# First attention of a gated cross-attention block: a pair's output transposed and summed by one product

## The chip, the cores and the metric

The kernel runs on one core of a Trainium2 chip. Its time is that of one execution on the device, in microseconds. TensorE multiplies matrices, VectorE, ScalarE and GpSimd work on tiles of 128 partitions, and SyncE and GpSimd issue most DMAs.

## The reference

Four blocks follow each other on 4 x 512 tokens of 512 channels: a cross-attention with int8 fake-quantised projections (16 heads of 32 channels), a mixture of experts, a second cross-attention, and a quantised feed-forward net. Every block adds `tanh(gate)` times its output to `x`. The change is in the core of the first attention:

```python
q = q.reshape(B, N, H, Dh)        # N = M = 512 tokens, H = 16, Dh = 32
attn = jax.nn.softmax(jnp.einsum('bnhd,bmhd->bhnm', q, k) * scale, axis=-1)
o = jnp.einsum('bhnm,bmhd->bnhd', attn, v).reshape(B, N, C)
```

## The kernel before

`l0_projections` writes q and k to DRAM, each as a high part (fp32r) and the low rest, and v as both parts side by side. `l0_attention` then works in 16 groups (`NG`): a batch element and four heads (`HG0`) each. A group has `UN` = 16 steps, one for a head and a tile of 128 queries, so 256 steps in all; two heads are a *pair*, 8 steps, 32 pairs in all.

What a step does, by engine:

- TensorE: `scores` (one product of 128 x 512 over the stacked high and low parts), `transposes` of the (unnormalised) probabilities (four of 128 x 128, float32, by a product with the identity), `values` (two products of 512 columns, high and low part of the probabilities, accumulated in the bank `pO` over the 8 steps of a pair). The stationary operand `vT` of `values` holds 128 columns: for a pair's two heads the high and the low part of v, 32 columns each, the rest zeros.
- VectorE: `maxima` (the negated row maximum of the scores) and `low` (low part of the transposed probabilities).
- ScalarE: `exps` (exponential with the row sums) and `high` (the high part, from the bank).

At the end of a pair, ScalarE copies `pO` to `Os` (`o_copy`): 128 rows, which are 2 heads x 2 parts x 32 channels, by 512 queries. TensorE transposes it into the bank `pR` (`o_transposes`, line 910, four of 128 x 128). VectorE inverts the row sums (`reciprocal`, line 970) and adds the two parts with a reduction over `w` (line 972, in 128 x 512, out 128 x 256) into `osum`. GpSimd multiplies `osum` with the inverse row sums into `O` (`scale_pair`, line 827), and SyncE stores `O` once a group is done.

The order on each engine is written out by `pipeline(eng, N, 2 * UN, stages)`: in step s every stage (function, lag) handles item s - lag, in the order of the list, and a hardware loop runs over turns of 32 steps, that is 4 pairs. TensorE's list is `(transposes, 3), (scores, 0), (values, 9), (o_transposes, 10)`, ScalarE's `(high, 3), (exps, 1), (o_copy, 9)`, VectorE's `(low, 4), (maxima, 0), (sum_parts, 10)`. Engines are tied by semaphores (`flag`s): a value product at a pair's start waits until `pO` has been copied (`oT_done`), and at a group's start for V (`v_in`, `v_zeroed`) too; `scores` and `transposes` reuse three banks each (`SB`, `TB` = 3), and `reuse` gives the distance, which at the loop's wrap is two items, not three.

GpSimd's queue runs in order: for each group k it first scales the two pairs of group k - 1, then waits until the scores have reached group k (`s_done`), issues a DMA that writes zeros to `rows`, and in groups 1 to 6 also loads constants and expert weights of the next stage (`load_constants`, `load_weights`, lines 808 and 809) and splits them. SyncE loads the stacks of q and k for group n (`load_stacks`) once the scores of group n - 2 are done.

Of the kernel before, what the change touches and what calls it, by code (L numbers as in the profile page):

```python
# [11 lines left out]
ALU = mybir.AluOpType  # L12
ACT = mybir.ActivationFunctionType
AX = mybir.AxisListType.X
# [656 lines left out]
def l0_attention(nc, g, t, written, shared):  # L671
# [10 lines left out]
    with Mem(nc, "b") as m:  # L682
# [11 lines left out]
        osum = m.sb("o_sum", [P, 2, QT, 2, DH0])  # L694
# [6 lines left out]
        pR = m.ps("pR", [P, QT, P])  # L701
# [12 lines left out]
        oT_done, oTr_done, summed, o_done = m.flag("oT"), m.flag("oTr"), m.flag("summed", 2), m.flag("o_done", depth=4)  # L714
# [3 lines left out]
        zeroed, z_out, v_zeroed = m.sem("zeroed"), m.sem("z_out"), m.sem("v_zeroed")  # L718
# [68 lines left out]
        def pair_end(r):  # L787

            return r % (2 * QT) == 2 * QT - 1

        def pair_buffer(r):
            return r // (2 * QT) % 2

        @block.gpsimd
        def _(pool):
            for b in range(2):
                nc.gpsimd.memset(V[:, b, :, 1::3].bitcast(F32), 0.0).then_inc(v_zeroed, 1)
            nc.gpsimd.memset(Z[:], 0.0).then_inc(zeroed, 1)
# [22 lines left out]
            def scale_pair(np):  # L821

                gb, pair = np // PAIRS % 2, np % PAIRS
                pool.wait_ge(summed.sem, summed.done(np))
                if pair == 0:
                    pool.wait_ge(o_out[gb], 16 + np // (2 * PAIRS) * 16)
                nc.gpsimd.tensor_tensor(O[:, gb, :, 2 * pair * DH0:2 * (pair + 1) * DH0].rearrange("p k (h c) -> p k h c", h=2),
                                        osum[:, np % 2],
                                        rinv[:, np % 2].rearrange("p h k -> p k h").unsqueeze(3).to_broadcast([P, QT, 2, DH0]),
                                        ALU.mult).then_inc(o_done.sem, 1)  # L830

            for k in range(NG):
                for pair in range(PAIRS):
                    if k >= 1:
                        scale_pair((k - 1) * PAIRS + pair)
# [22 lines left out]
            for pair in range(PAIRS):  # L858
                scale_pair((NG - 1) * PAIRS + pair)
# [4 lines left out]
        def _(pe):  # L864
# [37 lines left out]
            def o_transposes(i, r):  # L902
                if not pair_end(r):
                    return
                np = i * 2 * PAIRS + r // (2 * QT)
                pe.wait_ge(oT_done.sem, oT_done.done(np))
                pe.wait_ge(summed.sem, summed.past(np, 1))
                m.wait_apart(pe)
                for k in range(QT):
                    last = nc.tensor.transpose(pR[:, k], Os[:, pair_buffer(r), bass.ts(k, P)],  # L910
                                               g["ident"][:])
                last.then_inc(oTr_done.sem, 1)
# [34 lines left out]
        def _(dve):  # L947
# [14 lines left out]
            def sum_parts(i, r):  # L962

                if not pair_end(r):
                    return
                np = i * 2 * PAIRS + r // (2 * QT)
                gb, h, q = place(r)
                head = gb * HG0 + h - 1
                dve.wait_ge(o_done.sem, o_done.free(np))
                nc.vector.reciprocal(rinv[:, pair_buffer(r)], rsum[:, head:head + 2]).then_inc(summed.sem, 1)  # L970
                dve.wait_ge(oTr_done.sem, oTr_done.done(np))
                nc.vector.tensor_reduce(osum[:, pair_buffer(r)], pR[:].rearrange("p k (h w c) -> p k h c w", h=2, w=2),
                                        axis=AX, op=ALU.add).then_inc(summed.sem, 1)

            pipeline(dve, N, 2 * UN, [(low, 4), (maxima, 0), (sum_parts, 10)])
# [2741 lines left out]
```

## Time and profile before

| | |
|---|---|
| time, median of 3 runs | 3120.47 us (3116.66 to 3122.2) |
| the profiled execution | 3125.14 us |
| its span, first to last instruction | 3123.4 us |
| mean granted TensorE clock | 0.973 |
| VectorE busy | 2315.6 us (74% of the span) |
| ScalarE busy | 2083.3 us (67%) |
| GpSimd busy | 1416.3 us (45%) |

The span is what the trace covers; the execution's own time is a little longer. In the rows below, PE is TensorE and PEld its weight loads, DVE VectorE, ACT ScalarE, POOL GpSimd, SP SyncE. Tiles of this stage begin with `b_`: `b_pR` is the bank of the transposed output, `b_oT` is `Os`, `b_o_sum` is `osum`. An engine's instructions may overlap at their ends, so a duration is longer than the distance between two starts.

### The profile page before, as it was taken

The page shows a single profiled execution, that of the slowest core. Times are in us where ns is not written, and L with a number is a line of the kernel's source. Part 1 is how long each engine was busy: PE and PEld are TensorE (multiplying, and loading weights), DVE is VectorE, ACT ScalarE, POOL GpSimd, SP SyncE. Part 2 cuts the span into 40 slices and gives each one's busy share as a digit, 9 for nine tenths or more (in the row PEclk, how much of TensorE's full clock was granted, in tenths as well). Part 3 has the DMA queues.
Part 4 walks back from the last instruction along what each step waited for, and adds up shares of the span by engine and source line. Part 5 has one row for each costly group of instructions (what it writes and reads, how often), then busy time and mean ns, then how long its engine had stood idle before and what let it go on. Part 6 is the DMA issues. An engine that isn't in the chain of part 4 may idle for free. (4 is left out here: it accounts for less than half of the span.)

```text
span 3123.4 us, 56345 instructions
## 1 busy us (share of the span) xinstructions
PE 2916.9 (93%) x15383; PEld 2376.0 (76%) x15414; DVE 2315.6 (74%) x4667; ACT 2083.3 (67%) x4262; POOL 1416.3 (45%) x1793
## 2 busy tenths in 40 slices
PE   6969997887999999899999899999999999899988
PEld 4657775776888877788888688888888888688755
DVE  5679998755777658767676289888998988734377
ACT  4469996422666546566666588888888888633366
POOL 3413101312001075367687377777777777442132
PEclk9989998998999999999999999999999999999999
DMA  6898663216888586545456532332322322195410
GB/s 196 271 216 197 163 171 102 78 56 234 289 258 282 170 285 208 156 143 171 142 169 186 162 96 73 99 94 76 99 91 79 99 90 80 49 322 183 163 40 34
DMA packets 401823, 474.32 MB, mean 152 GB/s; under 512 B 52276, under 2 KB 267220, under 8 KB 401652
## 3 DMA queue, kind: packets, MB, share of 16 engines
q1 hardware_dynamic: 388692, 419.72, 44.6%
q0 software_dynamic: 12960, 52.61, 5.0%
q8 instruction: 72, 1.18, 0.2%
q14 instruction: 99, 0.81, 0.1%
HBM read 304.30 MB, written 167.92 MB: 151 GB/s over the span
## 5 line engine op out<-in xcount | busy, mean ns | idle before, releaser
L2869 POOL TENSOR_SCALAR h_probs<-h_exp,h_rowsum_inv 128x512 f32<-128x512 f32 x512 | 359.0, 701 | 277.4 <-PE h_pT L2717 260.9
L2797 DVE TENSOR_REDUCE h_neg_max<-h_scores 128x1 f32<-128x512 f32 x512 | 349.3, 682 | 145.5 <-PE h_scores L2709 145.4
L2759 ACT ACTIVATE h_exp<-h_scores,h_neg_max 128x512 f32<-128x512 f32 x512 | 355.7, 695 | 110.6 <-DVE h_neg_max L2797 100.9
L2810 DVE TENSOR_TENSOR h_probsT_lo<-h_pT,h_probsT_hi 128x512 fp32r<-128x512 f32 x512 | 348.1, 680 | 0.0
L2717 PEld LDWEIGHTS h_pT<-ident,h_probs 128*128 128x128 f32 x2048 | 255.8, 141 | 71.5 <-POOL h_probs L2869 1.8
L2717 PE MATMUL h_pT<-ident,h_probs 128*128 128x128 f32 x2048 | 307.3, 272 | 0.9 <-POOL h_probs L2869 0.8
L2768 ACT CAST h_probsT_hi<-h_pT 128x512 fp32r<-128x512 f32 x512 | 301.1, 588 | 0.9 <-PE h_pT L2717 0.9
L2985 PE MATMUL k_acc<-k_w_hi,k_cat 128*128 128x512 f32 x512 | 200.9, 392 | 12.3 <-POOL k_w_lo L3066 11.4
L2732 PE MATMUL h_pO<-h_probsT_hi,n_lo 128*128 128x512 f32 x512 | 203.3, 397 | 0.0
L2986 PE MATMUL k_acc<-k_w_lo,k_cat 128*128 128x512 f32 x512 | 200.4, 391 | 0.0
L925 ACT ACTIVATE b_probs<-b_scores,b_neg_max 128x512 f32<-128x512 f32 x256 | 184.2, 719 | 14.6 <-DVE b_neg_max L952 14.6
L952 DVE TENSOR_REDUCE b_neg_max<-b_scores 128x1 f32<-128x512 f32 x256 | 173.6, 679 | 20.4 <-PE b_scores L874 20.4
L2971 ACT CAST k_cat<-k_cat 128x512 fp32r<-128x512 bf16 x128 | 79.2, 621 | 161.5 <-PE k_acc L2986 143.3
L2554 DVE TENSOR_TENSOR g_normed<-g_pQ,g_rstd 128x512 f32<-128x512 f32 x160 | 110.2, 689 | 96.1 <-PE g_pT L2458 89.6
L934 ACT CAST b_probsT_hi<-b_pT 128x512 fp32r<-128x512 f32 x256 | 156.1, 610 | 29.4 <-PE b_pT L882 29.4
L959 DVE TENSOR_TENSOR b_probsT_lo<-b_pT,b_probsT_hi 128x512 fp32r<-128x512 f32 x256 | 173.5, 678 | 0.0
L2588 POOL TENSOR_TENSOR g_rstd<-g_var_eps,neg_half 128x4 f32<-128x4 f32 x160 | 166.3, 1039 | 13.5 <-POOL g_var_eps L2586 0.2
L2856 POOL TENSOR_TENSOR n_lo<-n_raw,n_hi_second 128x512 fp32r<-128x512 f32 x128 | 165.5, 1293 | 0.0
L882 PE MATMUL b_pT<-ident,b_probs 128*128 128x128 f32 x1024 | 156.1, 275 | 3.7 <-DVE b_probsT_lo L959 2.4
L2856 POOL TENSOR_TENSOR n_lo<-n_raw,n_hi_first 128x512 fp32r<-128x512 f32 x120 | 155.3, 1294 | 0.0
L882 PEld LDWEIGHTS b_pT<-ident,b_probs 128*128 128x128 f32 x1024 | 125.8, 142 | 38.8 <-issue 8.5
L2494 ACT ACTIVATE g_squares<-g_pQ 128x512 f32<-128x512 f32 x160 | 95.4, 597 | 83.8 <-PE g_pQ L2448 77.5
(460 smaller groups left out, 9051.3 us busy)
## 6 DMA issues: line engine op xcount, KB each, us to landing
e_w_raw<-in_w SPq DMA_DIRECT2D x24, 1792.0 KB, 8.1
lnT<-g_out SPq DMA_DIRECT2D x160, 256.0 KB, 2.3
n_raw<-lnT SPq DMA_DIRECT2D x64, 512.0 KB, 5.1
e_w_raw<-in_w SPq DMA_DIRECT2D x24, 896.0 KB, 9.9
n_raw<-lnT SPq DMA_DIRECT2D x64, 256.0 KB, 5.3
n_raw<-v SPq DMA_DIRECT2D x64, 256.0 KB, 5.6
cat<-h_cat SPq DMA_DIRECT2D x128, 128.0 KB, 1.8
k_cat<-cat SPq DMA_DIRECT2D x128, 128.0 KB, 4.4
```

Source lines behind the costliest of these rows:

```text
L882: last = nc.tensor.transpose(pT[r % TB][:, k], Pr[:, r % 4, bass.ts(k, P)], g["ident"][:])
L925: nc.scalar.activation(Pr[:, r % 4], pS[r % SB][:], ACT.Exp, bias=nmax[:, r % 4:r % 4 + 1], accum_out=rsum[:, gb * HG0 + h, q:q + 1]).then ...
L2717: last = nc.tensor.transpose(pT[r % 4][:, k], Pn[:, r % 4, bass.ts(k, P)], g["ident"][:])
L2732: nc.tensor.matmul(pO[h][:], vl, PTh[:, br * HPG + h, k], start=False, stop=(k == QT - 1)).then_inc(o_mm.sem, 1)
L2759: nc.scalar.activation(Pr[:, r % 4], pS[r % 2][:], ACT.Exp, bias=nmax[:, r % 4:r % 4 + 1], accum_out=rsum[:, r % 4:r % 4 + 1]).then_inc(ex ...
L2768: nc.scalar.copy(PTh[:, br * HPG + h, :, bass.ts(q, P)], pT[r % 4][:]).then_inc(hi_done.sem, 1)
L2797: v.tensor_reduce(nmax[:, r % 4:r % 4 + 1], pS[r % 2][:], axis=AX, op=ALU.max, negate=True).then_inc(nmax_done.sem, 1)
L2810: v.tensor_tensor(PTl[:, br * HPG + h, :, bass.ts(q, P)], pT[r % 4][:], PTh[:, br * HPG + h, :, bass.ts(q, P)], ALU.subtract).then_inc(lo_ ...
L2856: nc.gpsimd.tensor_tensor(Lo[:, gb, slot], Raw[:, gb, slot], Hi[gb][:, slot], ALU.subtract).then_inc(op_lo.sem, 1)
L2869: nc.gpsimd.tensor_scalar(Pn[:, r % 4], Pr[:, r % 4], rinv[:, r % 4:r % 4 + 1], 1.0, ALU.mult, ALU.mult).then_inc(norm_done.sem, 1)
L2985: nc.tensor.matmul(bank[:], lhsT, Wh[:, k], start=(k == 0), stop=False)
L2986: ins = nc.tensor.matmul(bank[:], lhsT, Wl[:, k], start=False, stop=(k == CK - 1))
```

## The change

The bank `pR` becomes half as wide, `[P, QT, 2, DH0]`. In place of four transposes TensorE makes four products (`nc.tensor.matmul`) of the same stationary operand with `fold`, a 128 x 64 float32 matrix: two identities of 32 for each head, one above the other, so that the product transposes and adds the two parts. `fold` is made once by GpSimd (a memset and two `affine_select`). `osum` and the reduction go. VectorE's `invert` computes the reciprocal at lag 8, and its new `scale_pair` at lag 10 multiplies `pR` with it straight into `O`. GpSimd no longer scales; the rest of its queue is as before. TensorE's wait before the products is now for the scaling of the pair before, and once for `fold`.

```diff
--- before.py
+++ after.py
@@ -691,14 +691,14 @@
         PTh = m.sb("probsT_hi", [P, HG0, QT, S], F32R)
         PTl = m.sb("probsT_lo", [P, HG0, QT, S], F32R)
         Os = m.sb("oT", [P, 2, S])
-        osum = m.sb("o_sum", [P, 2, QT, 2, DH0])
+        fold = m.sb("fold", [P, 2, DH0])
         nmax = m.sb("neg_max", [P, 4])
         rsum = m.sb("rowsum", [P, 2 * HG0, QT])
         rinv = m.sb("rowsum_inv", [P, 2, 2, QT])
         pS = [m.ps(f"scores{j}", [P, S]) for j in range(SB)]
         pT = [m.ps(f"pT{j}", [P, QT, P]) for j in range(TB)]
         pO = m.ps("pO", [P, S])
-        pR = m.ps("pR", [P, QT, P])
+        pR = m.ps("pR", [P, QT, 2, DH0])
 
         qk_in = [m.sem("qk_in0"), m.sem("qk_in1")]
         qk_first = m.sem("qk_first")
@@ -711,11 +711,11 @@
         s_done, nmax_done, tr_done = m.flag("scores"), m.flag("nmax"), m.flag("tr", depth=4)
         exp_done, hi_done, lo_done, o_mm = m.flag("exp", depth=6), m.flag("hi"), m.flag("lo", depth=6), m.flag("o_mm", depth=16)
 
-        oT_done, oTr_done, summed, o_done = m.flag("oT"), m.flag("oTr"), m.flag("summed", 2), m.flag("o_done", depth=4)
+        oT_done, oTr_done, inverted, o_done = m.flag("oT"), m.flag("oTr"), m.flag("inverted"), m.flag("o_done", depth=4)
         QK_LOADS = 8
         ZR = ROWS // NG
         Z = m.sb("zero", [P, ZR * D // P])
-        zeroed, z_out, v_zeroed = m.sem("zeroed"), m.sem("z_out"), m.sem("v_zeroed")
+        zeroed, z_out, v_zeroed, folds = m.sem("zeroed"), m.sem("z_out"), m.sem("v_zeroed"), m.sem("folds")
         block = m.block()
 
         def where(i, r):
@@ -795,6 +795,11 @@
         def _(pool):
             for b in range(2):
                 nc.gpsimd.memset(V[:, b, :, 1::3].bitcast(F32), 0.0).then_inc(v_zeroed, 1)
+            nc.gpsimd.memset(fold[:], 0.0).then_inc(folds, 1)
+            for part in range(2):
+                pool.wait_ge(folds, part + 1)
+                nc.gpsimd.affine_select(out=fold[:], in_=fold[:], compare_op=ALU.not_equal, fill=1.0, base=-part * DH0,
+                                        pattern=[[-2 * DH0, 2], [-1, DH0]], channel_multiplier=1).then_inc(folds, 1)
             nc.gpsimd.memset(Z[:], 0.0).then_inc(zeroed, 1)
             pool.wait_ge(zeroed, 1)
             rows = t["rows"].rearrange("n d -> (n d)")
@@ -818,21 +823,7 @@
                 pool.wait_ge(c_hi, k + 1)
                 nc.gpsimd.tensor_tensor(shared.c_low[:, k], Cr[:, k % 2], shared.c_high[:, k], ALU.subtract).then_inc(shared.c_lo, 1)
 
-            def scale_pair(np):
-
-                gb, pair = np // PAIRS % 2, np % PAIRS
-                pool.wait_ge(summed.sem, summed.done(np))
-                if pair == 0:
-                    pool.wait_ge(o_out[gb], 16 + np // (2 * PAIRS) * 16)
-                nc.gpsimd.tensor_tensor(O[:, gb, :, 2 * pair * DH0:2 * (pair + 1) * DH0].rearrange("p k (h c) -> p k h c", h=2),
-                                        osum[:, np % 2],
-                                        rinv[:, np % 2].rearrange("p h k -> p k h").unsqueeze(3).to_broadcast([P, QT, 2, DH0]),
-                                        ALU.mult).then_inc(o_done.sem, 1)
-
             for k in range(NG):
-                for pair in range(PAIRS):
-                    if k >= 1:
-                        scale_pair((k - 1) * PAIRS + pair)
                 pool.wait_ge(s_done.sem, s_done.depth + max(k * UN, UN // 2))
                 pool.dma_start(rows[k * ZR * D:(k + 1) * ZR * D].rearrange("(p a) -> p a", p=P), Z[:]).then_inc(z_out, 16)
                 if k == 1:
@@ -855,8 +846,6 @@
                                             ALU.mult, ALU.mult).then_inc(folded, 1)
                     nc.gpsimd.tensor_scalar(shared.bp[:], shared.bp[:], g["tanh_gates"][:, 0:1], 1.0,
                                             ALU.mult, ALU.mult).then_inc(folded, 1)
-            for pair in range(PAIRS):
-                scale_pair((NG - 1) * PAIRS + pair)
             pool.wait_ge(folded, 2)
             pool.wait_ge(z_out, 16 * NG)
 
@@ -904,11 +893,12 @@
                     return
                 np = i * 2 * PAIRS + r // (2 * QT)
                 pe.wait_ge(oT_done.sem, oT_done.done(np))
-                pe.wait_ge(summed.sem, summed.past(np, 1))
+                pe.wait_ge(o_done.sem, o_done.past(np, 1))
+                pe.wait_ge(folds, 3)
                 m.wait_apart(pe)
                 for k in range(QT):
-                    last = nc.tensor.transpose(pR[:, k], Os[:, pair_buffer(r), bass.ts(k, P)],
-                                               g["ident"][:])
+                    last = nc.tensor.matmul(pR[:, k].rearrange("p h c -> p (h c)"), Os[:, pair_buffer(r), bass.ts(k, P)],
+                                            fold[:].rearrange("p h c -> p (h c)"), start=True, stop=True)
                 last.then_inc(oTr_done.sem, 1)
 
             pipeline(pe, N, 2 * UN, [(transposes, 3), (scores, 0), (values, 9), (o_transposes, 10)])
@@ -959,7 +949,7 @@
                 nc.vector.tensor_tensor(PTl[:, h, :, bass.ts(q, P)], pT[r % TB][:],
                                         PTh[:, h, :, bass.ts(q, P)], ALU.subtract).then_inc(lo_done.sem, 1)
 
-            def sum_parts(i, r):
+            def invert(i, r):
 
                 if not pair_end(r):
                     return
@@ -967,12 +957,23 @@
                 gb, h, q = place(r)
                 head = gb * HG0 + h - 1
                 dve.wait_ge(o_done.sem, o_done.free(np))
-                nc.vector.reciprocal(rinv[:, pair_buffer(r)], rsum[:, head:head + 2]).then_inc(summed.sem, 1)
+                nc.vector.reciprocal(rinv[:, pair_buffer(r)], rsum[:, head:head + 2]).then_inc(inverted.sem, 1)
+
+            def scale_pair(i, r):
+
+                if not pair_end(r):
+                    return
+                np = i * 2 * PAIRS + r // (2 * QT)
+                gb, h, q = place(r)
+                dve.wait_ge(inverted.sem, inverted.done(np))
                 dve.wait_ge(oTr_done.sem, oTr_done.done(np))
-                nc.vector.tensor_reduce(osum[:, pair_buffer(r)], pR[:].rearrange("p k (h w c) -> p k h c w", h=2, w=2),
-                                        axis=AX, op=ALU.add).then_inc(summed.sem, 1)
-
-            pipeline(dve, N, 2 * UN, [(low, 4), (maxima, 0), (sum_parts, 10)])
+                if h == 1:
+                    dve.wait_ge(o_out[gb], 16 + i * 16)
+                nc.vector.tensor_tensor(O[:, gb, :, (h - 1) * DH0:(h + 1) * DH0].rearrange("p k (h c) -> p k h c", h=2), pR[:],
+                                        rinv[:, pair_buffer(r)].rearrange("p h k -> p k h").unsqueeze(3).to_broadcast([P, QT, 2, DH0]),
+                                        ALU.mult).then_inc(o_done.sem, 1)
+
+            pipeline(dve, N, 2 * UN, [(low, 4), (maxima, 0), (invert, 8), (scale_pair, 10)])
```

## Rows read from the trace of the kernel before

**Rows 1.** The page, its part 1: busy us (share of the span) xinstructions of each engine.
```profile
PE 2916.9 (93%) x15383; PEld 2376.0 (76%) x15414; DVE 2315.6 (74%) x4667; ACT 2083.3 (67%) x4262; POOL 1416.3 (45%) x1793
```

**Rows 2.** Windows, 320 to 360 us: us, busy time of engines, PEclk, DMA share, GB/s.
```profile
320.00:360.00 40.00, 36.94 (x227) 30.00 (x225) 38.89 (x69) 37.08 (x95) 3.61 (x6) 1.00 0.68 154
```

**Rows 3.** Timeline of a pair: start, us, engine, line, op, out<-in, count, [idle before <-releaser].
```profile
343.19 0.68 DVE L952 TENSOR_REDUCE b_neg_max<-b_scores 128x1 f32<-128x512 f32 x1
...
343.89 0.69 ACT L925 ACTIVATE b_probs<-b_scores,b_neg_max 128x512 f32<-128x512 f32 x1
...
344.57 0.58 ACT L942 COPY b_oT<-b_pO 128x512 f32<-128x512 f32 x1
...
345.20 0.50 PE L898 MATMUL b_pO<-b_probsT_hi,b_v 128*128 128x512 f32 x1
...
345.77 0.60 PE L910 MATMUL b_pR<-ident,b_oT 128*128 128x128 f32 x4
...
346.18 0.19 DVE L970 RECIPROCAL b_rowsum_inv<-b_rowsum 128x8 f32<-128x8 f32 x1
346.21 0.60 PE L882 MATMUL b_pT<-ident,b_probs 128*128 128x128 f32 x4
346.41 0.69 DVE L972 TENSOR_REDUCE b_o_sum<-b_pR 128x256 f32<-128x512 f32 x1
...
346.85 0.59 ACT L934 CAST b_probsT_hi<-b_pT 128x512 fp32r<-128x512 f32 x1 [0.53 <-PE b_pT L882]
```

**Rows 4.** Timeline of VectorE: the pairs' reductions over one turn of the loop.
```profile
314.97 0.69 DVE L972 TENSOR_REDUCE b_o_sum<-b_pR 128x256 f32<-128x512 f32 x1 [0.76 <-PE b_pR L910]
...
336.00 0.69 DVE L972 TENSOR_REDUCE b_o_sum<-b_pR 128x256 f32<-128x512 f32 x1 [0.26 <-PE b_pR L910]
...
357.53 0.69 DVE L972 TENSOR_REDUCE b_o_sum<-b_pR 128x256 f32<-128x512 f32 x1 [0.76 <-PE b_pR L910]
```

**Rows 5.** Timeline of ScalarE over four steps.
```profile
308.30 0.59 ACT L934 CAST b_probsT_hi<-b_pT 128x512 fp32r<-128x512 f32 x1
...
312.86 0.65 ACT L942 COPY b_oT<-b_pO 128x512 f32<-128x512 f32 x1
```

**Rows 6.** Groups by shape, VectorE: busy us, mean ns | idle before, releaser.
```profile
L972 DVE TENSOR_REDUCE b_o_sum<-b_pR 128x256 f32<-128x512 f32 x32 | 22.1, 692 | 13.0 <-PE b_pR L910 12.1
...
L1311 DVE TENSOR_TENSOR c_scores<-c_exps,c_rsum 128x128 f32<-128x128 f32 x1 | 0.3, 291 | 0.0
```

**Rows 7.** Timeline of weight loads, 543 to 545 us, and the line of the gate.
```profile
543.57 0.42 PEld L1456 LDWEIGHTS c_pH<-ident,c_h 128*128 128x128 f32 x4 [0.41 <-issue]
543.96 0.97 PEld L1466 LDWEIGHTS c_pL<-bc_gate_w,c_hT 128*128 128x128 f32 x8
...
L1466 PE MATMUL c_pL<-bc_gate_w,c_hT x128: 175/256/361, 544.1 to 648.1; 128*128 128x8 f32 x128
```

**Rows 8.** GpSimd's issues; DMA queues and landing in 214:222, in 300:320; a score product.
```profile
209.76 0.60 POOL L837 DMA_DIRECT2D rows<-b_zero  x1
...
215.16 0.54 POOL L809 DMA_DIRECT2D b_w_raw<-in_w  x1
...
q0 software_dynamic: 484, 1.67, 87.8%
q1 hardware_dynamic: 114, 0.19, 9.6%
...
b_k_stack<-qk SPq DMA_DIRECT2D x4, 256.0 KB, 14.8
...
b_k_stack<-qk SPq DMA_DIRECT2D x4, 256.0 KB, 8.3
...
215.95 0.50 PE L874 MATMUL b_scores<-b_k_stack,b_q_stack 128*128 128x512 f32 x1 [0.36 <-ACT b_probs L925]
```

**Rows 9.** Timeline, the stage's end.
```profile
522.05 0.69 DVE L972 TENSOR_REDUCE b_o_sum<-b_pR 128x256 f32<-128x512 f32 x1 [3.48 <-PE b_pR L910]
522.82 0.63 POOL L827 TENSOR_TENSOR b_o<-b_o_sum,b_rowsum_inv 128x256 f32<-128x256 f32 x1 [4.84 <-DVE b_o_sum L972]
```

## Prediction

> **What bounds the kernel now.** The share of busy time comes first: TensorE 93%, VectorE 74%, ScalarE 67% [rows 1]. That is an average over many stages and says nothing of the one that is edited, the first attention, from about 170 to 523 us. So the next view is the busy time in stretches: in 320 to 360 us VectorE works 38.89 of 40 us, ScalarE 37.08, TensorE 36.94, GpSimd 3.61, at a granted clock of full speed [rows 2]. All three big engines are nearly full and VectorE is the fullest.
>
> The timeline of one pair tells how they hang together [rows 3]. VectorE issues its instructions of 512 elements one slot after the other: from 343.19 to 346.18 there are five in 2.99 us, so a slot is 0.598 us (a row's duration, 0.68, overlaps the next). A pair has 8 steps, each with one maximum and one low part: 16 slots, 9.57 us. To these come the reciprocal, slot 0.24 (346.18 to 346.41), and the reduction, slot 0.60. Full speed is thus 10.41 us a pair. Measured: from the reduction at 314.97 to that at 357.53, four pairs, one turn of the loop, 42.56 us [rows 4]. 4 x 10.41 is 41.64; the missing 0.91 is the reduction waiting for the pair's transposes: nothing in pairs one and three, some 0.20 beyond the reciprocal's slot in the second (idle 0.26 in the row) and 0.71 in the fourth (idle 0.76).
>
> Why it waits is a chain that starts at the end of a maximum, t0 = 343.78 [rows 3]: exponential at 343.89 (+0.11), copy of the output at 344.57 (+0.79), the next pair's first value product at 345.20 (+1.42), the four transposes at 345.77 (+1.99) and 0.60 long, reduction at 346.41 (+2.63). VectorE itself gets there after two steps and the reciprocal: 4 x 0.598 + 0.24 = +2.63. The two arrive together: even in the good pairs this chain has no slack. In pairs two and four TensorE has two more waits queued between copy and value product (new V loaded, zeros written), and the chain is some 0.2 longer. In the fourth ScalarE is also about 0.5 behind: at the loop's wrap the three banks are reused at distance two instead of three, and ScalarE makes up only 0.053 a step, its step being (312.86 - 308.30) / 4 = 1.14 against VectorE's 1.196 [rows 5].
>
> **The change part by part.**
>
> *VectorE: a reduction of 512 goes, a multiplication of 256 comes.* No row has a tensor-by-tensor product of 256 elements. One of 128 takes 0.291 [rows 6], one of 512 some 0.68 [rows 3]. On the straight line between them, (0.68 - 0.29) / 384 = 0.001 an element, 256 take 0.42, and less the 0.08 of overlap that is a slot of 0.34. Bounds of the slot 0.21 and 0.60, the slots of the two rows; I take 0.33. Gain 0.27 a pair.
>
> *The reciprocal moves two steps earlier.* It still costs its slot of 0.24 but now inside the two steps between t0 and the scaling. It goes from the place just ahead of the reduction to a place just behind t0, so VectorE still arrives at t0 + 2.63. No gain, no loss. Bounds 0 and 0.24.
>
> *TensorE: four transposes become four float32 products of 64 columns.* This step decides. A float32 product that is no transpose and no fp32r occurs once in the trace: the gate logits, 16 tiles x 4 calls = 64 products, but 128 records of product, and as many of weight load. Each product is worked in two records with a weight load each. Their pace [rows 7]: four weight loads of a transpose and eight of the gate follow each other; the four start at 543.57 and the eight at 543.96, 0.10 a load; the eight last 0.97, one load 0.19, so they start (0.97 - 0.19) / 7 = 0.11 apart, although their products move only 8 columns. So the weight load sets the pace, for a transpose as for each half of a product, and 64 columns against 128 save nothing. Four transposes of the pair hold TensorE 0.44 (345.77 to 346.21) [rows 3], eight records 0.88. The chain grows by 0.44. Bounds: 0, if half as many columns at half a record's price gave it back, and 0.6, if the 64 columns stand beside the load and not under it.
>
> The Trainium skill ("FP8 and Floating Point Precision", TensorE Precision Notes) says that true FP32 takes four passes through the array. By passes alone a product here would be 4 x 64 = 256 column cycles, an estimate of 0.107 us at 2.4 GHz, as long as a transpose's 0.11, and the chain would not grow; that is the first rival. The trace shows two records rather than four and two weight loads, which the rule does not count; by the rows it is 0.22 a product.
>
> *What the longer chain does to VectorE.* It waits 0.44 longer at each pair and works 0.27 less: +0.17 a pair. There is a second-order part. After the pair's products TensorE's next transposes (346.21) and ScalarE's cast behind them (346.85) come 0.44 later, while VectorE's maximum two slots on comes only 0.17 later. Now the cast at 346.85 sets the exponential after next at 346.85 + 0.46 + 1.14 = 348.45 (an exponential's slot is 344.57 - 343.89 = 0.68 and leaves 0.46 of 1.14 to the cast), and the maximum that it needs ends at 346.41 + 0.60 + 0.60 + 0.68 = 348.29: ScalarE is some 0.15 behind. It will be 0.42 behind, makes up 5 x 0.053 = 0.27 until the next t0 and starts the next chain 0.15 late. Waits then: 0.44 + 0.15 = 0.59 in pairs one and three, 0.79 in the second, 0.71 + 0.44 = 1.15 in the fourth (there the wrap sets ScalarE back anyway): 3.12 a turn. A turn: 4 x (9.57 + 0.24 + 0.33) + 3.12 = 43.68, against 42.56: +1.1. Eight turns' worth of pairs: **+9 us**. Without the second-order part +5.5. TensorE does not become the bound: 36.94 of 40 us [rows 2] is 9.8 a pair of 10.64, and 10.3 after, under 10.9.
>
> *GpSimd loses 32 scalings of 0.63.* They lie beside everything but the last and save nothing, it is mostly idle [rows 2]. But its queue is in order, and each group's scalings stood ahead of the group's DMAs: zeros of 624 KB and, with group one, the constants and two chunks of weights. These were issued at 209.76 to 215.7 [rows 8]; without scalings ahead they wait for the scores alone and go out some 15 us earlier, at about 194 (one group, half of 42.56, before 215.95), together with the stacks of group two. What such a meeting does is seen in the trace a group later: between 214 and 222 us the GpSimd queue holds 87.8% of the DMA engines and SP's 9.6%, and a k stack took 14.8 us to land instead of 8.3 [rows 8]. Stacks issued until about 200 us would land at 214 to 219; they are needed at 215.95, where the first score product of group two now starts without waiting for a DMA. Price 0 to 5 us, once; I take 1.5. Later groups have only zeros and one chunk of weights there, and the same 21 us to land.
>
> *Small things.* Two semaphore waits more, one on TensorE (folds), under the value products; and one on VectorE (store two groups back), in half of the pairs, behind its own wait: nothing taken, up to 0.06 x 16 = 1. The fold matrix is made by GpSimd while the first stacks load, and needed ten steps later: free. At the stage's end the last reduction starts at 522.05 and the scaling on GpSimd ends at 523.45 [rows 9]; after, the start is 0.44 later and 0.42 follows, so 522.91, some 0.5 us sooner.
>
> **Sum.** 9 + 1.5 - 0.5 = +10 us in the profiled execution, which took 3125.14 with a span of 3123.4. That run lies 4.7 above the median of 3120.47 (3116.66 to 3122.2); the difference is put on the median: **3130 us**.
>
> **The rivals.**
>
> *The products cost no more than the transposes* (ends on the other side). If the eight records run at 0.055, or a product is one record, the chain keeps its 2.63 and VectorE gets the whole 0.27: 32 x 0.27 = 8.6, and 0.9 at the end, less 0 to 1.5 for the DMAs: 3111 to 3112. It decides from a chain growth under 0.27 a pair. For it: half of the columns, and the count of passes. Against it: the eight gate records of 8 columns each at the pace of a load. Chance 12%.
>
> *Grown chain, but nothing else.* ScalarE keeps up and the DMAs fit: +5.5 - 0.5, 3125 to 3126. For it: ScalarE does catch up within a pair in three of four pairs now. Against it: its step is 1.14 against 1.196, so a pair gives back only 0.4. Chance 22%.
>
> *The stacks of group two land late.* The +9 and a stop of 4 to 6 us near 216: 3134 to 3136. For it: the queue shares at 214 to 222. Against it: only one group is struck. Chance 16%, the rest of 50% being the forecast.
>
> **How the numbers follow.** What can be told from no change is 0.2%, 6.2 us: 3114.2 to 3126.7. The first rival is faster (12%). The second lies within (22%). Forecast and late stacks are slower (66%). The range goes from 3121, under the second rival and with run-to-run spread, to 3137; the first rival is left out below.
>
> **What would show it.** The bank's products have 256 records instead of 128 and hold TensorE some 0.88 a pair. VectorE's scaling lasts 0.42, and ahead of each stands an idle of 0.5 to 1.2, some 25 us in all against 12.1 before [rows 6]. A turn is 43.7 us. GpSimd waits for score products alone, its DMAs of group one go out near 194, and it is to be seen whether the score product of group two waits for a stack. I am wrong if the scaling follows with no idle (then the products are cheap), or if the turn is under 42.

## The result, and the profile after

| | before | after |
|---|---|---|
| time, median (range, runs) | 3119.36 us (3114.39 to 3125.55, 8) | 3130.32 us (3127.07 to 3132.73, 8) |
| ratio, after to before | | 1.0035 (95%: 1.0024 to 1.0045) |
| profiled execution, its span | 3125.14, 3123.4 us | 3132.36, 3130.7 us |
| first score product to last store issued | 169.0 to 523.47: 354.5 us | 168.7 to 535.28: 366.6 us |
| one turn of the loop, four pairs | 42.56 us | 44.05 us |

The changed kernel is slower, by 0.35%; 3130 us was forecast. The stage of the change grew by 12.1 us. The profiled executions lie only 7.2 apart, because the rest of the kernel, which the change does not touch, was 4.8 us shorter in this one.

Busy time by engine, the page of after, against [rows 1]:

```profile
PE 2926.5 (93%) x15511; PEld 2389.3 (76%) x15542; DVE 2309.4 (74%) x4667; ACT 2081.3 (66%) x4262; POOL 1394.0 (45%) x1764
```

VectorE has lost 6 us and GpSimd 22; TensorE has 128 product records more. In stretches, against [rows 2] (us, busy time of PE, PEld, DVE, ACT, POOL, PEclk, DMA share, GB/s):

```profile
320.00:360.00 40.00, 37.86 (x238) 31.42 (x238) 37.05 (x66) 35.83 (x91) 1.12 (x2) 1.00 0.68 159
```

VectorE worked 38.89 of 40 us before and works 37.05 now, ScalarE 35.83 instead of 37.08, TensorE 37.86 instead of 36.94, at the same clock. Two engines idle more and the stage is longer: what grew is a chain between them. Everything that touches the bank `pR` in after (records: min/median/max ns, first and last start, shape; then the idle of the engine before the scaling, by what ended it):

```profile
L900 PEld LDWEIGHTS b_pR<-b_fold,b_oT x256: 187/192/193, 196.5 to 534.4; 128*128 128x128 f32 x128
L900 PE MATMUL b_pR<-b_fold,b_oT x256: 217/275/295, 196.7 to 534.4; 128*128 128x64 f32 x128
L972 DVE TENSOR_TENSOR b_o<-b_pR,b_rowsum_inv x32: 424/425/426, 197.9 to 534.8; 128x256 f32<-128x256 f32 x32
...
  PE b_pR L900: 24.9, 23
  issue: 9.5, 10
```

256 product records of 64 columns where 128 of 128 columns stood, and as many weight loads. The scaling lasts 0.425 us, and VectorE idled 34.4 us ahead of it (24.9 + 9.5); ahead of the reduction it was 13.0 [rows 6]. One pair in the timeline of after, to be laid beside [rows 3]:

```profile
283.59 0.68 DVE L942 TENSOR_REDUCE b_neg_max<-b_scores 128x1 f32<-128x512 f32 x1
...
284.19 0.19 DVE L960 RECIPROCAL b_rowsum_inv<-b_rowsum 128x8 f32<-128x8 f32 x1
...
284.85 0.69 DVE L942 TENSOR_REDUCE b_neg_max<-b_scores 128x1 f32<-128x512 f32 x1
...
284.99 0.58 ACT L932 COPY b_oT<-b_pO 128x512 f32<-128x512 f32 x1
...
285.61 0.50 PE L887 MATMUL b_pO<-b_probsT_hi,b_v 128*128 128x512 f32 x1 [0.66 <-ACT b_oT L932]
...
286.19 1.00 PE L900 MATMUL b_pR<-b_fold,b_oT 128*128 128x64 f32 x8
...
287.03 0.61 PE L871 MATMUL b_pT<-ident,b_probs 128*128 128x128 f32 x4
...
287.40 0.42 DVE L972 TENSOR_TENSOR b_o<-b_pR,b_rowsum_inv 128x256 f32<-128x256 f32 x1 [0.67 <-PE b_pR L900]
```

Count from the end of the maximum that starts at 283.59, t0 = 284.19 (its slot is 0.60). The copy starts at t0 + 0.80, the next pair's value product at +1.42, the products of the pair at +2.00: to 0.01 as before (+0.79, +1.42, +1.99). The eight records hold TensorE until 287.03, 0.84 us, where four held it 0.44. The scaling starts at +3.21 instead of +2.63. One turn on VectorE, the scalings and two of the low parts that follow, against [rows 4]:

```profile
276.44 0.42 DVE L972 TENSOR_TENSOR b_o<-b_pR,b_rowsum_inv 128x256 f32<-128x256 f32 x1 [1.25 <-PE b_pR L900]
277.00 0.69 DVE L949 TENSOR_TENSOR b_probsT_lo<-b_pT,b_probsT_hi 128x512 fp32r<-128x512 f32 x1
...
298.37 0.42 DVE L972 TENSOR_TENSOR b_o<-b_pR,b_rowsum_inv 128x256 f32<-128x256 f32 x1 [0.91 <-PE b_pR L900]
298.71 0.68 DVE L949 TENSOR_TENSOR b_probsT_lo<-b_pT,b_probsT_hi 128x512 fp32r<-128x512 f32 x1
...
309.19 0.42 DVE L972 TENSOR_TENSOR b_o<-b_pR,b_rowsum_inv 128x256 f32<-128x256 f32 x1 [0.77 <-issue]
...
320.49 0.42 DVE L972 TENSOR_TENSOR b_o<-b_pR,b_rowsum_inv 128x256 f32<-128x256 f32 x1 [1.24 <-PE b_pR L900]
```

Where the engines waited between 200 and 500 us (us in total, times, longest), in after:

```profile
ACT b_probsT_hi L924 <- PE b_pT L871: 30.1, 34, 1.3
DVE b_o L972 <- PE b_pR L900: 19.1, 20, 1.3
...
PE b_pO L887 <- ACT b_oT L932: 15.9, 20, 1.0
```

and in before:

```profile
ACT b_probsT_hi L934 <- PE b_pT L882: 20.4, 35, 0.7
PE b_pO L898 <- ACT b_oT L942: 16.1, 21, 0.9
...
DVE b_o_sum L972 <- PE b_pR L910: 7.0, 14, 0.8
```

TensorE's wait for the copy of the output is the same in both. VectorE's wait for `pR` and ScalarE's for the next transposes, which stand behind the products in TensorE's queue, grew. GpSimd's DMAs of group one, and the first score product of group two, against [rows 8]:

```profile
192.99 0.54 POOL L828 DMA_DIRECT2D rows<-b_zero  x1 [8.11 <-PE b_scores L863]
...
217.67 0.49 PE L863 MATMUL b_scores<-b_k_stack,b_q_stack 128*128 128x512 f32 x1 [1.59 <-DMA b_k_stack<-qk]
```

And the end of the stage, against [rows 9]:

```profile
534.83 0.42 DVE L972 TENSOR_TENSOR b_o<-b_pR,b_rowsum_inv 128x256 f32<-128x256 f32 x1 [4.00 <-PE b_pR L900]
535.28 0.40 SPq L772 DMA_DIRECT2D o<-b_o  x1
```

### The profile page after: what moved, and what is told of

It reads as the page before. It is cut to its first block and busy times, and to the rows that moved or that the text cites. A ratio compares the mean times of both kernels' runs of the same rounds, so it can differ in the third digit from the quotient of the medians.

```text
span 3130.7 us, 56594 instructions
## 1 busy us (share of the span) xinstructions
PE 2926.5 (93%) x15511; PEld 2389.3 (76%) x15542; DVE 2309.4 (74%) x4667; ACT 2081.3 (66%) x4262; POOL 1394.0 (45%) x1764
## 5 line engine op out<-in xcount | busy, mean ns | idle before, releaser
L924 ACT CAST b_probsT_hi<-b_pT 128x512 fp32r<-128x512 f32 x256 | 158.5, 619 | 41.5 <-PE b_pT L871 41.4
```

## The experiments

Times are medians with the number of runs. The kernel before ran beside them, and each ratio is to those runs: its median was 3120.73 us beside e1 to e4, 3122.72 beside f1 to f4 and 3123.04 beside g1 to g4, so times of different rounds are compared by their ratios. "A turn" is four pairs from the middle of the stage, between about 270 and 365 us of the profile, unless other times are given. Diffs are against after unless they say otherwise.

**Scaling one step later (e1).**

```diff
-pipeline(dve, N, 2 * UN, [(low, 4), (maxima, 0), (invert, 8), (scale_pair, 10)])
+pipeline(dve, N, 2 * UN, [(low, 4), (maxima, 0), (invert, 8), (scale_pair, 11)])
```

> The changed kernel with VectorE's scaling one step later (lag 11 in place of 10): VectorE does two more slots (1.20 us) before it asks for the pair's products. Theory (the chain exponential, copy, value product, eight product records is what VectorE waits for, and nothing else is full): the waits of 0.58, 0.83, 0.68 and 1.15 us a turn go, a turn falls from 44.05 to 40.6 to 41.2 us, the kernel to about 3130 - 8 x 3.0 = 3106 us (3102 to 3110). Rival (TensorE has become the bound with 128 more records): the wait moves to the maxima or low parts, a turn stays above 43 us, the time at 3127 or more.

3128.42 us (9 runs), ratio 1.0025 (1.0015 to 1.0036); a turn 44.00. The theory, 3106 us and 40.6 to 41.2, failed, and the rival's conditions were met. VectorE's timeline and its waits from 200 to 500 us:

```profile
340.18 0.69 DVE L942 TENSOR_REDUCE b_neg_max<-b_scores 128x1 f32<-128x512 f32 x1 [1.00 <-PE b_scores L863]
340.78 0.41 DVE L972 TENSOR_TENSOR b_o<-b_pR,b_rowsum_inv 128x256 f32<-128x256 f32 x1
...
DVE b_neg_max L942 <- PE b_scores L863: 26.7, 28, 1.3
```

The scaling waits for nothing any more, and the idle stands ahead of the maximum before it: 26.7 us, where in after 24.7 stood ahead of the scaling (19.1 put down to `pR`, 5.6 to issue). Where the scaling stands in VectorE's order is not what costs: the scores stand in TensorE's queue behind the products too, and the maximum that needs them comes as late as the scaling did. This is a second path from the products to VectorE, as long as the first.

**The same for the reduction of before (e2).** `(sum_parts, 10)` becomes `(sum_parts, 11)`, in before.

> The kernel before with its reduction one step later (lag 11), reciprocal with it. Theory: only 0.91 us a turn was waiting there, a turn falls from 42.56 to 41.64 us, the kernel by 7 us to about 3112. With e1 it also tells what the change is worth once the chain is covered: 4 x (0.60 - 0.34) = 1.04 us a turn. Rival (the pairs' waits in the kernel before come from a bound on ScalarE or TensorE that will show elsewhere): a turn stays at 42.4 or more, within 2 us of 3119.

3122.79 us (10 runs), ratio 1.0007 (0.9997 to 1.0016). A turn is 43.11, 0.55 longer, where 41.64 was expected: ahead of the maxima are waits of 0.94, 0.23, 0.39 and 0.24. Why later is worse here stayed open. VectorE's timeline settles something else:

```profile
348.22 0.19 DVE L970 RECIPROCAL b_rowsum_inv<-b_rowsum 128x8 f32<-128x8 f32 x1
348.33 0.64 DVE L972 TENSOR_REDUCE b_o_sum<-b_pR 128x256 f32<-128x512 f32 x1
348.88 0.68 DVE L959 TENSOR_TENSOR b_probsT_lo<-b_pT,b_probsT_hi 128x512 fp32r<-128x512 f32 x1
```

The same reciprocal and reduction in the same order, with the products long done, take 0.66 us together (348.22 to 348.88). In the kernel before they took 0.84 in the pairs that showed no idle (346.18 to 347.02). So 0.18 of the reciprocal's "slot" of 0.24 was a wait for the transposes, in every pair.

**Transposes kept, direct scaling kept (e3).** The four transposes of before, and VectorE scales the high parts alone: the sum of the parts is left out.

```diff
-pR = m.ps("pR", [P, QT, 2, DH0])
+pR = m.ps("pR", [P, QT, P])
...
-last = nc.tensor.matmul(pR[:, k]..., Os[:, pair_buffer(r), bass.ts(k, P)], fold[:]..., start=True, stop=True)
+last = nc.tensor.transpose(pR[:, k], Os[:, pair_buffer(r), bass.ts(k, P)], g["ident"][:])
...
-nc.vector.tensor_tensor(O[...], pR[:], rinv[...], ALU.mult)
+nc.vector.tensor_tensor(O[...], pR[:].rearrange("p k (h w c) -> p k h w c", h=2, w=2)[:, :, :, 0], rinv[...], ALU.mult)
```

> The changed kernel with the four transposes by the identity back (bank of 128 columns) and VectorE scaling 256 elements straight from the bank; the low parts are left out of the sum. VectorE and GpSimd are as in the changed kernel, only TensorE's records go back from eight to four. Theory (the records are what made it slower): waits fall by 0.44 us a pair and ScalarE's lag with them, a turn is 4 x (9.57 + 0.24 + 0.34) + 0.9 = 41.5 us, the kernel 3119 - 8 + 1 = 3112 us (3109 to 3116). Rival (the direct scaling from the bank, or its place, costs the time): a turn stays near 44 us, 3127 or more.

3119.26 us (10 runs), ratio 0.9996 (0.9984 to 1.0009). The bank has 128 product records again. VectorE's scalings:

```profile
313.07 0.43 DVE L972 TENSOR_TENSOR b_o<-b_pR,b_rowsum_inv 128x256 f32<-128x256 f32 x1 [0.84 <-PE b_pR L900]
...
355.49 0.43 DVE L972 TENSOR_TENSOR b_o<-b_pR,b_rowsum_inv 128x256 f32<-128x256 f32 x1 [0.83 <-PE b_pR L900]
```

A turn is 42.42, 1.63 under after, but only 0.14 under before. The products cost what was thought; VectorE's saved time bought next to nothing: 41.5 us a turn and 3112 us were expected, and the turn missed by 0.9.

**The four transposes of before done twice (e4).**

```diff
-for k in range(QT):
+for k in [*range(QT), *range(QT)]:
     last = nc.tensor.transpose(pR[:, k], Os[:, pair_buffer(r), bass.ts(k, P)], g["ident"][:])
```

> The kernel before with the pair's four transposes made twice, eight records in place of four, all else as before. Theory: the chain alone grows by 0.44 us, VectorE keeps its slot of 0.60; from 42.56 a turn goes by 4 x 0.44 and about 0.5 to 0.9 of ScalarE's lag to 44.8 to 45.2 us, the kernel by 18 to 21 us to about 3138. Rival (TensorE has slack that takes the longer row of records): a turn stays under 43.2 us, under 3125.

3133.84 us (4 runs), ratio 1.0044 (1.0027 to 1.0061). Records and reductions:

```profile
L910 PE MATMUL b_pR<-ident,b_oT x256: 270/272/299, 197.7 to 535.9; 128*128 128x128 f32 x128
...
320.65 0.69 DVE L972 TENSOR_REDUCE b_o_sum<-b_pR 128x256 f32<-128x512 f32 x1 [1.15 <-PE b_pR L910]
...
364.88 0.69 DVE L972 TENSOR_REDUCE b_o_sum<-b_pR 128x256 f32<-128x512 f32 x1 [1.16 <-PE b_pR L910]
```

A turn is 44.23: four records more a pair, and nothing else, cost 1.67, or 0.42 a pair. The forecast of 44.8 to 45.2 and about 3138 us was too high by the lag of ScalarE, 0.5 to 0.9 a turn, that it had added: there is none here. With the reduction, and the scaling still on GpSimd, this kernel's turn is 0.18 longer than that of after.

**The products ahead of the value products (f1).** In TensorE's list `(o_transposes, 10)` goes ahead of `(values, 9)`.

> The changed kernel with the pair's eight product records ahead of the next pair's first value product in TensorE's list, in place of behind it. First theory (VectorE's scaling waits for the chain copy, value product, records): the chain loses the 0.57 us of the value product, a turn falls from 44.05 to about 42 us, 3114 us. Second theory, formed after the scaling at lag 11 had changed nothing (TensorE's in-order queue is what ends last: it stops for the copy, and all that stands behind it up to the next scores comes late by the records): the same work stands between copy and next scores, a turn stays at 43.7 to 44.2, within 3 us of 3130.

3129.37 us (10 runs), ratio 1.0026 (1.0014 to 1.0038), a turn 43.98: no change, as the second theory said; the first, 42 us and 3114, failed. Between 200 and 500 us TensorE now waits for the copy ahead of the records, 16.4 us (in after 15.9 ahead of the value product), VectorE's idle ahead of the scalings falls from 24.7 to 19.4, and ScalarE waits for the transposes behind as long as before, 30.7 (30.1). The scaling is served earlier, and it gains nothing: what stands behind both comes as late.

**ScalarE's copy ahead of the exponential, in after (f2) and before (f3).**

```diff
-pipeline(act, N, 2 * UN, [(high, 3), (exps, 1), (o_copy, 9)])
+pipeline(act, N, 2 * UN, [(high, 3), (o_copy, 9), (exps, 1)])
```

> The changed kernel with ScalarE's copy of the output ahead of the exponential of its step, not behind it. Second theory (TensorE's queue stops for the copy): the copy starts 0.55 to 0.68 us earlier, the stop shrinks by as much in each pair, and a turn falls by 1.2 to 2.2, from 44.05 to 41.9 to 42.9 us, the kernel by 10 to 17 us to 3113 to 3120. Rival (TensorE's own work of 9.9 us a pair and its drains are the bound, the stop is only slack): a turn stays above 43.5, over 3126.

> The kernel before with the same exchange on ScalarE. There only 0.91 us a turn was waiting: second theory 42.56 falls to 41.64 to 42.0, the kernel by 4 to 7 us to 3112 to 3116. Rival: no change within 2 us.

After so changed: 3127.61 us (10 runs), ratio to before 1.0014 (1.0002 to 1.0025), a turn 43.12, between the 41.9 to 42.9 expected and the rival's 43.5. Before so changed: 3120.74 us (10 runs), ratio 0.9991 (0.9982 to 1.0001), a turn 42.28, above the 41.64 to 42.0 expected; its time can't be told from no change. The scalings of f2:

```profile
319.32 0.42 DVE L972 TENSOR_TENSOR b_o<-b_pR,b_rowsum_inv 128x256 f32<-128x256 f32 x1 [0.69 <-PE b_pR L900]
...
340.01 0.42 DVE L972 TENSOR_TENSOR b_o<-b_pR,b_rowsum_inv 128x256 f32<-128x256 f32 x1 [0.27 <-PE b_pR L900]
...
351.69 0.42 DVE L972 TENSOR_TENSOR b_o<-b_pR,b_rowsum_inv 128x256 f32<-128x256 f32 x1 [0.67 <-PE b_pR L900]
...
362.44 0.42 DVE L972 TENSOR_TENSOR b_o<-b_pR,b_rowsum_inv 128x256 f32<-128x256 f32 x1 [0.69 <-PE b_pR L900]
```

Two pairs together take 20.69 us with eight records a pair; the pair at the wrap takes 11.68, the next 10.75. In f3, with four records, the four pairs take 10.28, 10.23, 11.24 and 10.53. An earlier copy is worth 0.93 a turn in after and 0.28 in before: of the 1.49 that lay between them 0.84 is left, and most of that in the pair at the wrap and the one behind it (0.66 of it). That the reuse of the banks holds these two up is argued from their place, not shown.

**The copy first, products at lag 11, scaling at lag 12 (f4).**

> The changed kernel with the copy ahead of the exponential, the pair's products one step later (lag 11) and the scaling two steps later (lag 12): the value products of the stopped step, then the next step's transposes and scores go ahead of the eight records. Second theory: the stop and the records no longer add up ahead of one score product; a turn falls to 40.6 to 41.5 us (VectorE full: 4 x 10.15), the kernel to 3103 to 3110, faster than the kernel before. Rival (TensorE's work is the bound): a turn of 43 us or more.

3121.35 us (10 runs), ratio 1.0002 (0.9988 to 1.0016). A turn 42.85, above the 40.6 to 41.5 expected, and the kernel is not faster than before, where 3103 to 3110 was expected: pairs of 10.34 to 10.43 and one of 11.70 at the wrap.

**GpSimd's DMAs held back as before (g1).** Ahead of the zeros' DMA of each group k from 1 on, GpSimd waits until the scaling has got there:

```diff
+                if k >= 1:
+                    pool.wait_ge(o_done.sem, o_done.depth + k * PAIRS)
                 pool.wait_ge(s_done.sem, s_done.depth + max(k * UN, UN // 2))
```

> The changed kernel with GpSimd waiting for the scalings of the group before (as it did when it made them) ahead of each group's zeros, constants and weights. Theory (the early DMAs of group one hold up the stacks of group two, once): the first score product of group two no longer waits for a stack (1.59 us there in the changed kernel), the stage ends 1 to 1.5 us sooner, a turn stays at 44.05; the time is 0 to 2 us under 3130 and cannot be told by itself. Rival (the early DMAs disturb every group): a turn falls by 0.3 or more.

3133.18 us (10 runs), ratio 1.0027 (1.0014 to 1.0041), a turn 44.02. GpSimd's first DMA of group one, and the first score product of group two:

```profile
208.00 0.54 POOL L830 DMA_DIRECT2D rows<-b_zero  x1 [25.01 <-PE b_scores L865]
...
214.74 0.50 PE L865 MATMUL b_scores<-b_k_stack,b_q_stack 128*128 128x512 f32 x1 [0.38 <-ACT b_probs L917]
```

They go out 15 us later and the wait for the stack is gone; counted from the first pair the stage is 1.3 us shorter. In the time that can't be told (3133.18 is higher than after's 3130.32, with a before of 3123.04 beside it instead of 3119.36).

**Products in fp32r (g2).** `Os` and `fold` become fp32r, so the output is rounded before its parts are added.

> The changed kernel with the copied output and the fold matrix as fp32r, which rounds the output before it is summed; nothing else differs. Theory (a float32 product is worked in two records with a weight load each, and their number is the price): 128 records in place of 256, four to a pair at 0.11 us or a little more; a turn falls from 44.05 to 42.4 to 42.6, as with the four transposes (42.42), and the kernel to 3118 to 3121. Rival (64 columns in fp32r run as slow as the two records): a turn stays above 43.5, 3128 or more.

3120.84 us (10 runs), ratio 0.9993 (0.9982 to 1.0004). The bank's records and two scalings a turn apart:

```profile
L903 PEld LDWEIGHTS b_pR<-b_fold,b_oT x128: 186/190/192, 195.1 to 519.5; 128*128 128x128 f32 x128
L903 PE MATMUL b_pR<-b_fold,b_oT x128: 192/276/278, 195.3 to 519.6; 128*128 128x64 f32 x128
...
314.60 0.42 DVE L975 TENSOR_TENSOR b_o<-b_pR,b_rowsum_inv 128x256 f32<-128x256 f32 x1 [0.75 <-PE b_pR L903]
...
356.81 0.42 DVE L975 TENSOR_TENSOR b_o<-b_pR,b_rowsum_inv 128x256 f32<-128x256 f32 x1 [0.75 <-PE b_pR L903]
```

128 records for 128 products, one weight load each, and a turn of 42.21 (42.4 to 42.6 expected, and 3118 to 3121 us): the second record is a matter of float32, not of the narrow product.

**The copy first and a longer loop (g3, g4).** f4 with g1's wait and the engines' loops over 96 steps, so that three banks wrap without a shorter distance (g3); before with the same loops (g4).

> The changed kernel with the copy ahead of the exponential, products at lag 11, scaling at lag 12, GpSimd's DMAs late again, and loops of 96 steps on the three compute engines, so that the three banks are never reused at distance two at the loop's wrap. Theory (with copy first and late products, 1.3 of 42.85 us a turn is the wrap): four pairs take 4 x 10.38 = 41.5 us everywhere, the stage ends 10 us before that of the kernel with copy first and lag 11 alone, the kernel is at 3110 to 3113, faster than the kernel before. Rival (the longer loop's code has to be fetched and stops the engines, or the wrap was not the cause): four pairs still take 42.5 or more, 3120.

> The kernel before with loops of 96 steps on the three compute engines, nothing else. Theory (0.71 of the 0.91 us a turn of waiting came from the wrap): four pairs take 41.9 to 42.0 in place of 42.56, the kernel 4 to 5 us less. Rival: code fetches take it back, within 2 us of the kernel before.

g3: 3120.04 us (12 runs), ratio 0.9997 (0.9986 to 1.0009), where 3110 to 3113 was expected. g4: 3123.8 us (12 runs), ratio 1.0003 (0.9993 to 1.0013), where 4 to 5 us less were expected. These loops have two turns, so they jump once. VectorE in g3, at the loop's jump and away from it:

```profile
317.46 0.41 DVE L978 TENSOR_TENSOR b_o<-b_pR,b_rowsum_inv 128x256 f32<-128x256 f32 x1
320.03 0.69 DVE L955 TENSOR_TENSOR b_probsT_lo<-b_pT,b_probsT_hi 128x512 fp32r<-128x512 f32 x1 [2.16 <-ACT b_probsT_hi L930]
...
329.73 0.41 DVE L978 TENSOR_TENSOR b_o<-b_pR,b_rowsum_inv 128x256 f32<-128x256 f32 x1
...
433.08 0.41 DVE L978 TENSOR_TENSOR b_o<-b_pR,b_rowsum_inv 128x256 f32<-128x256 f32 x1
...
464.04 0.41 DVE L978 TENSOR_TENSOR b_o<-b_pR,b_rowsum_inv 128x256 f32<-128x256 f32 x1
```

And VectorE in g4, at its jump:

```profile
311.83 0.69 DVE L976 TENSOR_REDUCE b_o_sum<-b_pR 128x256 f32<-128x512 f32 x1 [0.21 <-PE b_pR L914]
...
315.55 0.69 DVE L963 TENSOR_TENSOR b_probsT_lo<-b_pT,b_probsT_hi 128x512 fp32r<-128x512 f32 x1 [3.03 <-issue]
...
328.65 0.69 DVE L976 TENSOR_REDUCE b_o_sum<-b_pR 128x256 f32<-128x512 f32 x1 [0.61 <-PE b_pR L914]
```

Away from the jump three pairs of g3 take 30.96 us, 10.32 each, and four of g4 41.83 (370.66 to 412.49), close to the 41.9 to 42.0 of its theory, where before takes 42.56: the wrap's cost of about 0.7 a turn is gone. Whether the reuse at distance two made it or the jump itself stays open, since away from the jump both are gone. The jump that is left eats the gain. In g3 two pairs take 12.98 and 12.27, some 4.6 us more than two others; in g4 one takes 16.82, some 6.2 more. Each engine's first instruction behind the jump in g4 comes after an idle that the profile puts down to nothing ("issue"): 4.27 us on TensorE (316.06), 3.03 on VectorE, 1.92 on ScalarE. After it TensorE's granted clock is 0.50, its lower level of 1.2 GHz, from 316 to 320 us. That fits the rival, code that has to be fetched, but no run shows the fetch. In g3 the wait of group two for its stacks came back as well (1.94 us, at 236.71), with GpSimd's DMAs late.

## Why the prediction was right

The four kernels of a two by two table, by the distance from t0 to the reduction or scaling in each pair of a turn, read off as above (first, second, third pair after the wrap, pair at the wrap):

| | chain, four pairs | sum | the rest of the turn | turn |
|---|---|---|---|---|
| before: 4 records, reduction | 2.62, 2.83, 2.62, 3.34 | 11.41 | 31.15 | 42.56 |
| e3: 4 records, direct scaling | 2.80, 3.03, 2.92, 3.38 | 12.13 | 30.29 | 42.42 |
| e4: 8 records, reduction | 3.06, 3.23, 3.07, 3.74 | 13.10 | 31.13 | 44.23 |
| after: 8 records, direct scaling | 3.19, 3.45, 3.31, 3.78 | 13.73 | 30.32 | 44.05 |

The distances differ by up to 0.02 from one turn to the next; the pair shown above has 3.21.

- **TensorE, four float32 products: +0.44 a pair.** Right, and shown three ways: e4 has +0.42 with nothing else changed, after is 0.41 a pair above e3, and with one record a product (g2) it is gone. 64 columns save nothing: the eight hold TensorE 0.84 us. By an estimate from the four passes that the Trainium skill ("FP8 and Floating Point Precision", TensorE Precision Notes) gives for true FP32, a product of 64 columns would take 0.107 us and four would be no longer than four transposes. The trace does not agree: the eight records take 0.84 us, 0.21 a product, and after is slower than e3.
- **VectorE's own saving: 0.27 a pair.** Right as a slot: 0.34 by its rows (298.37 to 298.71) against 0.60, so 0.26. At the loop's wrap the low part follows after 0.56 (276.44 to 277.00) instead of 0.34, in e3 too (0.54); behind the reduction nothing of it shows. So the rest of the turn fell by 0.81 to 0.86, not 1.08. The 0.2 belongs to the loop's jump: this scaling is the last instruction of VectorE's turn, and behind the seventh and last turn, where nothing jumps back, the low part follows after 0.34 again (496.54 to 496.88).
- **The reciprocal: no gain.** Right in effect, wrong in size, from a misread row. It takes 0.06 (284.19 to 284.85, less 0.60), not 0.24, and e2 shows that it took no more in before: the other 0.18 was VectorE waiting. So the sentence "the two arrive together" was wrong. VectorE was there at least 0.18 early in every pair, its own work was 4 x 10.23 us a turn and not 4 x 10.41, and 1.64 us a turn of before was waiting, not 0.91. The chain set the time of every reduction already. For after it means 0.18 a pair less of work and as much more of waiting than forecast: the four idles of a turn sum to 3.59 (0.67, 0.91, 0.77, 1.24), with overlaps some 0.3 more, where waits of 3.12 were forecast. In all 34.4 us of idle stood ahead of the scalings, where some 25 was said.
- **The second-order part.** The forecast chain was 2.63 + 0.44 + 0.15 = 3.22, then 3.42, 3.22 and 3.78, sum 13.64; measured 13.73. Its size was right and its cause half right. It comes from the shorter scaling and not from the longer products: e4 grows by 0.40 to 0.45 in every pair, e3 by 0.18, 0.20, 0.30 and 0.04 with no record added. Only in the third pair does it begin at ScalarE, as the step said (copy at t0 + 0.96 instead of 0.79). In the second the value product comes 0.15 later, behind a copy that is on time; and in the first it is the start of the scaling, 0.20 after the modelled end of the last product instead of 0.04 [rows 3]. What lies behind these two wasn't found out.
- **The path: half of it.** The sum takes the whole cost from VectorE's longer wait at the scaling. That wait is there, but it is not the only path. With the scaling one step later (e1) it waits for nothing, and with the products ahead of the value product (f1) it waits less, yet a turn stays at 44.00 and 43.98. The same eight records also stand in TensorE's queue ahead of the next transposes and scores, which the prediction used for ScalarE's lag alone; by this path the next maximum comes as late. Both paths carry the same eight records, so the number could come out. That TensorE has no slack left is not shown either: it is busy 37.86 of 40 us and stops for the copies besides, but the ends of its records are modelled, and an earlier copy (f2) still gains 0.93 a turn.
- **A turn: 43.68 forecast, 44.05 measured.** The mis-sized terms are the 0.2 at the wrap and 0.09 of chain; the rest is the slot of 0.34 for 0.33, four times, and rounding. Over the distance from the first pair to the last, 31 of 32 pairs, 1.49 a turn is 11.5 us, where +9 was written.
- **DMAs of group one: 1.5 us.** Right: issued from 192.99 on (about 194 said), stack waited for 1.59, stage 1.3 shorter without (g1). e3 and g2 have such a wait as well, of 1.7 and 2.70.
- **The end: -0.5.** Right: from the last pair's first product to the last store it takes 1.64 us (533.64 to 535.28), and in before 2.09 (521.38 to 523.47). 12.1 less 11.5 and 1.3 leaves -0.7 for this and for the filling of the pipeline.
- **The rivals.** "The products cost no more" was false, but its price was false as well: e3 and g2 are kernels in which they cost no more, and they stand at 0.9996 and 0.9993, not at 3111. Its price took VectorE's saving whole and left out the lag that the forecast itself charged. In e3 the rest of the turn falls by 0.86, and the chain takes 0.72 of it back. "Grown chain, but nothing else" makes a turn of 43.24, and fell by the 44.05 and by e3, where the chain grows with no record added. "Late stacks" wanted a stop of 4 to 6 us and fell by the 1.59 (its 3134 to 3136 also leaves out the -0.5 of the end).

So the median came out at 3130 partly by luck: the stage grew by 12.1 and not by 10, the medians lie 10.96 apart, and the forecast was put on a before of 3120.47, which is 3119.36 beside after. That the records decide, and their price, was right and is shown. How much of a pair VectorE works and how much it waits was not: 0.18 us a pair were counted as work and are waiting, and the two errors cancel in the sum.

## What to carry to other kernels

Before work is moved from one engine to another, write out the chain from one event of a pair to the next, and every second path past it, and see how much of the period is chain and how much is the engine's own queue; a saving on the fullest engine is worth what its partners can follow, here 0.14 of 1.04 us a turn. A short instruction ahead of one that waits hides part of the wait in its slot, as the reciprocal did; look at its price where nothing behind it waits. Count a small float32 product as two products with a weight load each, unless it is a transpose or fp32r; 64 and 8 columns cost the same here. When a wait only changes its place as an instruction is moved back, as in e1, look for the engine whose queue holds both.

## What the runs showed of the hardware

- A float32 product of 128 x 64 has two records of 0.275 us, some 0.105 us apart, with a weight load of 0.192 each; in fp32r it has one.
- A reciprocal of 8 columns takes 0.06 us of VectorE's time, between two instructions of 512 and ahead of a reduction that waits for nothing (e2) alike.
- A tensor-by-tensor product of 128 x 256 from a bank takes 0.425 us, and the next starts 0.34 after it, or 0.54 to 0.56 where the loop's jump lies between.
- With loops of 96 steps the one jump cost some 4.6 us in g3 and 6.2 in g4, against 0.2 on VectorE at a jump of the loop of 32 steps.
